# Per-token head attention: softmax along the free dimension, 32x32 block transposes, and score products with two tokens stationary

## The reference

```python
x = x + clip(layer0(x * style0) * demod0 + bias0, -256, 256)
kx = layerK(x)                       # reshaped to 16 heads of 32
scores = einsum("bnhd,bnjd->bnhj", kx, kx) / sqrt(32)
A = softmax(scores, axis=-1)
out = einsum("bnhj,bnjd->bnhd", A, kx)
x = x + layerO(out)
```

## Time and profile before

| | us |
|---|---|
| median of three runs | 892.17 |
| lowest and highest of them | 884.9, 893.84 |
| the profiled execution | 884.66 |
| its span, first to last instruction | 882.9 |
| TensorE busy in it | 820.0 |

### The profile page before, as it was taken

One profiled execution on the slowest core, in us unless ns is written; L12 is line 12 of the kernel. 1 busy time (PEld: TensorE's weight loads), 2 busy tenths in 40 slices (PEclk: granted clock), 3 DMA queues, 4 the chain that ended last, 5 costly groups with the idle time before them and its releaser, 6 DMA issues.

```text
span 882.9 us, 25721 instructions
## 1 busy us (share of the span) xinstructions
PE 820.0 (93%) x11024; PEld 794.0 (90%) x11024; DVE 613.6 (70%) x1224; ACT 548.3 (62%) x1077; POOL 11.6 (1%) x8
## 2 busy tenths in 40 slices
PE   5977989899999999999999999999999999997764
PEld 5976979899999999999999999999999999996664
DVE  4634675877787778778777877777777787774351
ACT  3433555666667767677666777666776667763452
POOL 3100000000000000000000000000000000000000
PEclk9888999999999999999999999999999999999788
DMA  8034366566666666666665666666666666654323
GB/s 267 25 90 100 79 147 157 142 160 160 141 149 145 145 157 164 161 147 165 150 160 129 165 138 148 159 161 164 144 161 153 155 134 160 139 125 107 73 73 119
DMA packets 471233, 123.95 MB, mean 140 GB/s; under 512 B 403152, under 2 KB 468816, under 8 KB 471120
## 3 DMA queue, kind: packets, MB, share of 16 engines
q1 hardware_dynamic: 471120, 122.31, 57.0%
HBM read 55.16 MB, written 50.33 MB: 119 GB/s over the span
## 4 chain that ended last, share of the span: by engine, by line
PE 80%; DMA 7%; DVE 4%; SPq 3%; ACT 3%; issue 1%; ACTq 0%; DVEq 0%
PE lin_ps L367 56%; PE s_ps L407 14%; PE y_ps L429 6%; PE cd_ps L414 3%; SPq L257 2%; DMA k_turned<-kx 2%; DMA yr<-y_turned 2%; DMA k_bd<-k_rhs 2%; DMA k_st<-k_turned 1%; PE y_ps L390 1%; SPq L265 1%; DVE k_rhs L701 1%; ACT y L548 1%; ACT y_hi L474 1%; PE y_ps L378 1%
## 5 line engine op out<-in xcount | busy, mean ns | idle before, releaser
L367 PE MATMUL lin_ps<-x_hi,w_hi 128*128 128x256 f32 x1024 | 297.6, 291 | 9.2 <-DVE x_lo L651 4.8
L367 PE MATMUL lin_ps<-x_lo,w_hi 128*128 128x256 f32 x1024 | 293.1, 286 | 0.0
L367 PE MATMUL lin_ps<-x_hi,w_lo 128*128 128x256 f32 x1024 | 292.9, 286 | 0.0
L367 PEld LDWEIGHTS lin_ps<-x_hi,w_hi 128*128 128x128 f32 x1024 | 199.5, 195 | 17.4 <-issue 11.6
L367 PEld LDWEIGHTS lin_ps<-x_lo,w_hi 128*128 128x128 f32 x1024 | 199.7, 195 | 1.6
L367 PEld LDWEIGHTS lin_ps<-x_hi,w_lo 128*128 128x128 f32 x1024 | 199.8, 195 | 0.0
L651 DVE SCALAR_TENSOR_TENSOR x_lo<-x,style,x_hi 128x256 fp32r<-128x256 f32 x256 | 111.8, 480 | 80.8 <-ACT x_hi L474 80.8
L367 PE MATMUL lin_ps<-y_hi,w_hi 128*128 128x256 f32 x512 | 148.2, 289 | 14.3 <-DVE y_lo L651 14.3
L407 PE MATMUL s_ps<-k_rhs,k_bd 128*64 128x48 f32 x4096 | 136.3, 226 | 12.0 <-DMA k_bd<-k_rhs 9.5
L367 PE MATMUL lin_ps<-y_lo,w_hi 128*128 128x256 f32 x512 | 147.3, 288 | 0.0
L367 PE MATMUL lin_ps<-y_hi,w_lo 128*128 128x256 f32 x512 | 146.9, 287 | 0.0
(11 more groups left out here) (58 smaller groups left out, 812.4 us busy)
## 6 DMA issues: line engine op xcount, KB each, us to landing
x<-xT SPq DMA_DIRECT2D x32, 512.0 KB, 5.3
k_turned<-kx SPq DMA_DIRECT2D x32, 512.0 KB, 3.7
k_st<-k_turned SPq DMA_DIRECT2D x128, 128.0 KB, 2.9
k_bd<-k_rhs SPq DMA_DIRECT2D x128, 128.0 KB, 4.0
y_turned<-y SPq DMA_DIRECT2D x128, 128.0 KB, 2.5
yr<-y_turned SPq DMA_DIRECT2D x32, 512.0 KB, 5.4
outT<-o SPq DMA_DIRECT2D x31, 512.0 KB, 2.9
p_bd<-wT SPq DMA_DIRECT2D x4, 512.0 KB, 7.2
```

The source lines that it names most:

```text
L367: mm = pe.matmul(lin_ps[:, n % NLB, 0:T], w[:, k, m * P:(m + 1) * P], r[:, k, :], start=(q == 0), stop=(q == len(passes) - 1))
```

## The change

**Scores.** Two tokens of each of four token blocks are stationary: 32 columns of k_rhs. The streaming operand is two tokens of the four parts of k_bd, 128 columns. Four such products fill the four groups of 32 partitions of one PSUM bank. The identity columns are gone. k_bd now holds its four parts one after the other, so a partition of a part is one run. Half of the computed 16x16 blocks belong to unlike tokens; ScalarE takes the even groups times a mask, and VectorE adds the odd groups times another mask, which leaves 16 scores in a row of sc.

**Softmax.** Maximum, subtraction, exponential, sum, reciprocal and multiplication run along the row of 16. Then a 32x32 block transpose on VectorE brings the probabilities into the layout of the products. The products of TensorE with ones, the splits and the corrected reciprocal are gone. The eight masked copies are four on VectorE and four on ScalarE in all chunks.

**Values.** k_rhs goes to DRAM and back in four transfers (`v_to_dram`, `v_from_dram`), and two block transposes on VectorE turn it into v_sb (`turn_v`).

**Order.** The accumulators of the linear layers get a fourth bank. The lists of all engines are written anew: SyncE's round, the place of turn_k, of the evacuation of y and of the next chunk's high and low parts. In the head layer L0 of chunk 3 is ahead of the scores of chunk 0. Three small constant inputs are no longer loaded.

```diff
         def pe_steps(i):
-            return (blocks(L0, i, [0, 1]) + one("max", i - 2) + blocks(L0, i, [2, 3])
-                    + blocks(O, i - 4, [0, 1]) + one("sum", i - 2) + blocks(O, i - 4, [2, 3])
-                    + blocks(K, i) + score_units(i - 1) + one("pv", i - 2))
-
-
-        SHARED_P = N - 2
+            return blocks(L0, i) + blocks(O, i - 4) + blocks(K, i) + one("scores", i - 1) + one("pv", i - 2)
...
+            + blocks(K, 0, [1, 2, 3]) + blocks(L0, 2) + blocks(K, 1) + blocks(L0, 3) + one("scores", 0)
+            + blocks(K, 2) + one("scores", 1) + blocks(K, 3) + one("pv", 0) + blocks(L0, 4) + one("scores", 2)
+            + blocks(K, 4) + one("pv", 1) + blocks(O, 0) + one("scores", 3) + one("pv", 2))
...
+            blocks(L0, last) + blocks(O, last - 4, [0, 1]) + blocks(K, last) + one("scores", last - 1)
+            + one("pv", last - 2) + blocks(O, last - 4, [2, 3]) + blocks(O, last - 3) + one("scores", last)
+            + one("pv", last - 1) + blocks(O, last - 2) + one("pv", last) + blocks(O, last - 1) + blocks(O, last))
...
             def spread_k(c):
...
                 if c == 0:
                     sp.wait_ge(g_zero, 1)
                 sp.wait_ge(v_krhs, c + 1)
-                for tb in range(HR):
-                    sp.dma_start(k_bd[HD * tb:HD * (tb + 1), :, tb, :],
-                                 k_rhs[HD * tb:HD * (tb + 1), 0]).then_inc(ld_kbd, DMA)
+                for r in range(R):
+                    sp.dma_start(k_bd[HD * r:HD * (r + 1), r], k_rhs[HD * r:HD * (r + 1)]).then_inc(ld_kbd, DMA)
+
+            def v_to_dram(c):
+                sp.wait_ge(v_krhs, c + 1)
+                if c >= 2:
+                    sp.wait_ge(v_in_landed, DMA * CT * (c - 1))
+                sp.dma_start(v_dram[c % 2], k_rhs[:, :, :].rearrange("p w n -> p (w n)")).then_inc(v_out_landed, DMA)
+
+            def v_from_dram(c):
+                sp.wait_ge(v_out_landed, DMA * (c + 1))
+                if c:
+                    sp.wait_ge(v_v, c)
+                src = v_dram[c % 2].rearrange("(r d) (c s) -> d r c s", d=HD, c=CT)
+                for ct in range(CT):
+                    sp.dma_start(k_v[HD * ct:HD * (ct + 1)].rearrange("p r x n -> p r (x n)"),
+                                 src[:, :, ct]).then_inc(v_in_landed, DMA)
...
+            for i in range(DEPTH + 1, N):
+                k_to_dram(i - 1)
+                k_from_dram(i - 1)
+                y_to_dram(i - 3)
+                y_from_dram(i - 3)
+                if i < N - 2:
                     load_x(i + 2)
-                if i >= 1:
-                    k_to_dram(i - 1)
-                    k_from_dram(i - 1)
-                if i >= 3:
-                    y_to_dram(i - 3)
-                if i >= 1:
-                    spread_k(i - 1)
-                if i >= 3:
-                    y_from_dram(i - 3)
-                if 3 <= i < N - 2:
-                    load_x(i + 2)
-                if DEPTH <= i < last:
+                spread_k(i - 1)
+                v_to_dram(i - 1)
+                if i < last:
                     store(i - 4, 0, 1)
+                v_from_dram(i - 1)
...
-                for q in range(GJ):
-                    for u in range(2):
-                        g = j * W + 2 * q + u
-                        mm = pe.matmul(s_ps[64 * u:64 * u + 64, j % 2, q * NC:(q + 1) * NC],
-                                       k_bd[:, g].rearrange("p b n -> p (b n)"), k_rhs[:, :, g, :], start=True, stop=True)
...
+            def scores(c):
+
+                pe.wait_ge(ld_kbd, DMA * R * (c + 1))
+                if c:
+                    pe.wait_ge(v_sc, c)
+                for x in range(2):
+                    for q in range(QS // 2):
+                        for ct in range(CT):
+                            w = (ct * 2 + x) * QS + 2 * q
+                            mm = pe.matmul(s_ps[HD * ct:HD * (ct + 1), x, q * P:(q + 1) * P],
+                                           k_rhs[:, w:w + 2].rearrange("p w n -> p (w n)"),
+                                           k_bd[:, :, w:w + 2].rearrange("p r w n -> p r (w n)"),
+                                           start=True, stop=True)
...
             def pv(c):
                 pe.wait_ge(v_pbd, c + 1)
-                if c >= SHARED_P:
-                    pe.wait_ge(a_pbd, c - SHARED_P + 1)
+                pe.wait_ge(a_pbd, c + 1)
+                pe.wait_ge(v_v, c + 1)
                 if c == 0:
                     pe.wait_ge(a_norm, 3)
-                for q in range(GJ):
-                    if q % PB == 0 and c:
-                        pe.wait_ge(a_y, NPB * (c - 1) + q // PB + 1)
-                    for j in range(HR):
-                        grp = j * GJ + q
+                else:
+                    pe.wait_ge(a_y, 2 * c)
+                for q in range(QS):
+                    for j in range(4):
+                        hi, x = j // 2, j % 2
+                        grp = ((x * QS // 2 + q // 2) * 2 + hi) * 2 + q % 2
                         mm = pe.matmul(y_ps[HD * j:HD * (j + 1), q // PB, (q % PB) * P:(q % PB + 1) * P],
-                                       sv_sb[:, c % 2, grp, HEADS:NC],
+                                       v_sb[:, c % 2, j * QS + q],
...
+            def even_scores(c):
+                if c == 0:
                     act.wait_ge(v_wlo, 6)
                     act.wait_ge(g_wsq, 2)
-                act.wait_ge(pe_s, SU * c + j + 1)
-                act.activation(sv_sb[:, c % 2, j * GJ:(j + 1) * GJ, :],
-                               s_ps[:, j % 2, 0:GJ * NC].rearrange("p (g n) -> p g n", n=NC),
-                               ACT.Copy).then_inc(a_sv, 1)
-
-            def evacuate_y(c, k):
-                if c and k == 0:
+                    act.wait_ge(v_odd, 1)
+                else:
+                    act.wait_ge(v_pt, c)
+                act.wait_ge(pe_s, c + 1)
+                act.activation(sc[:], s_ps[:, :, :].rearrange("p x (g o n) -> p (x g) o n", o=2, n=HEADS)[:, :, 0],
+                               ACT.Copy, scale=odd_mask[:, 0:1]).then_inc(a_even, 1)
+
+            def evacuate_y(c, l):
+                if c and l == 0:
                     act.wait_ge(y_out_landed, DMA * HR * c)
-                act.wait_ge(pe_pv, NPB * c + k + 1)
-                act.activation(y_sb[:, :, :, k * 2 * PB:(k + 1) * 2 * PB].rearrange("p h b w -> p w b h"),
-                               y_ps[:, k, :].rearrange("p (w b h) -> p w b h", b=HR, h=HEADS),
+                act.wait_ge(pe_pv, c + 1)
+                act.activation(y_sb[:, :, l].rearrange("p h (c q) -> p h c q", c=CT),
+                               y_ps[:, :, :].rearrange("p b (q c l h) -> p l h c (b q)", c=CT, l=2, h=HEADS)[:, l],
...
             def spread_some(c):
 
-                act.wait_ge(v_prob, c + 1)
-                act.wait_ge(pe_pv, NPB * c)
+                act.wait_ge(v_pt, c + 1)
+                act.wait_ge(pe_pv, c)
                 for t in range(TG // 2, TG):
-                    a = act.activation(p_bd[:, :, t, :], prob[:], ACT.Copy, scale=tok_mask[:, t:t + 1])
+                    a = act.activation(p_bd[:, :, t, :], p_turned[:], ACT.Copy, scale=tok_mask[:, t:t + 1])
...
+                    (c3, evacuate_y, 0), (c3, evacuate_y, 1), (c0, l0_out, 0), (c2, exponentials), (c0, l0_out, 1),
+                    (c0, l0_out, 2), (c2, spread_some), (c0, l0_out, 3), (c0, x1_hi_of, 0),
+                    (c4, o_out, 0), (c0, x1_hi_of, 1), (c4, o_out, 1), (i + 1, x_hi_of, 0),
+                    (c4, o_out, 2), (i + 1, x_hi_of, 1), (c4, o_out, 3),
+                    (c0, k_out, 0), (c3, y_hi_of, 0), (c0, k_out, 1), (c3, y_hi_of, 1), (c0, k_out, 2),
+                    (c0, k_out, 3), (c1, even_scores)]
...
             def turn_k(c):
-                dve.wait_ge(k_in_landed, DMA * HR * (c + 1))
+                dve.wait_ge(k_in_landed, DMA * R * (c + 1))
                 if c:
-                    dve.wait_ge(pe_s, SU * c)
-                dve.tensor_copy(k_rhs[:, 0], k_st[:, :, :].rearrange("p n w -> p w n")).then_inc(v_krhs, 1)
+                    dve.wait_ge(pe_s, c)
+                    dve.wait_ge(v_out_landed, DMA * c)
+                dve.tensor_copy(k_rhs[:].rearrange("p (c x q) n -> p c x q n", c=CT, x=2),
+                                k_st[:].rearrange("p n (x c q) -> p c x q n", x=2, c=CT)).then_inc(v_krhs, 1)
+
+            def turn_v(c):
+                if c == 0:
+                    dve.wait_ge(g_wsq, 2)
+                    dve.wait_ge(v_wlo, 6)
+                dve.wait_ge(v_in_landed, DMA * CT * (c + 1))
+                if c >= 2:
+                    dve.wait_ge(pe_pv, c - 1)
+                for hi in range(2):
+                    v = dve.transpose(v_sb[:, c % 2, hi * NG // 2:(hi + 1) * NG // 2],
+                                      k_v[:, 2 * hi:2 * hi + 2].rearrange("p l x n -> p x l n"))
+                v.then_inc(v_v, 1)
...
+            def merge_scores(c):
```

(35 more changed lines are left out.)

331 lines of the change are left out of this document (123 added, 208 removed).

## The result

The changed kernel takes 829.28 us (median of four runs, 827.42 to 835.37) against 891.1 (884.9 to 893.84), a ratio of 0.9327 with a 95% interval of 0.9255 to 0.9399. It is 7% faster. The forecast was 755 with a range of 730 to 800, so half of the gain that I counted on is missing, and the time lies outside the range. The profiled execution took 827.42 us, with a span of 825.6.

What follows compares the result with a forecast made beforehand. TensorE was taken to bound the middle of the run. Span 882.9 less 77 (25 rounds), 27.6 (head) and 28 (tail) gave 750, with 1.8 for execution 752, with scatter 755 us; range 730 to 800.

Steps and rivals of the forecast that it cites:

- walk through a round: Middle rounds, timed from TensorE's first linear layer: all hand-overs just fit; 0.1 us for small waits makes the round 21.25 us.
- the sum of SyncE's queue: SyncE's serial queue in a middle round: issues and landings sum to 20.4 us, under TensorE's 21.16.
- the landing of the spread: Spread of k into k_bd: first issue at 12.8 us, last landed near 16.8, wanted by the scores at 17.2.
- a late start is caught up before the spread: SyncE's queue: a late start does no harm, because k has landed by about 7 us and is wanted at 11.6.
- rival (b): Spread of k in the rounds: k_bd stays late, 1.9 us a round more, giving 802 us; chance 0.08.
- TensorE's own round: Middle rounds: TensorE's 24.34 us less 2.26 for scores and 0.92 for maxima and sums, 21.16 us.
- VectorE's transposes: Softmax and values on VectorE: three 32x32 transposes a round at 0.69 us each, 2.07 in all.
- Rival (a): Coupled middle round: a step of the walk about 1 us later, 1.2 us a round, 785 us; chance 0.22.
- (c): VectorE: a transpose costs many times a copy; at 4.5 us each, 934 us, slower than before; chance 0.02.
- (d): Scores on TensorE don't shrink: 2.2 us a round and 16 at the ends more, 825 us; chance 0.04.
- the identity in k_rhs: Head: writing it stands on the chain for 3.88 us, which go; counted as 3.9 of 27.6 us saved.
- the tail: After the rounds: walk of the last chunk gives 71 us, taken as 72 instead of 99.9, so 28 saved.

Runs made afterwards that it cites:

- experiment 3: Changed kernel with the spread of k issued for chunk 0 only, later scores computed from chunk 0's k_bd; 760.73 us (one run).
- experiment 6: Changed kernel with v loads one round later, load of x behind the spread of k, and copy of k early in VectorE's round; 763.43 us, ratio 0.860.
- experiment 2: Changed kernel with the four v loads of a chunk issued one round later in SyncE's queue, behind the next chunk's k out; 773.88 us, ratio 0.8742.
- experiment 7: Changed kernel with only VectorE's copy of k moved ahead of the second half of x1, SyncE's list untouched; 833.66 us, ratio 0.9366.
- experiment 10: Kernel of experiment 6 with SyncE's head list rewritten: y of chunk 0 and k of chunk 4 sent as soon as they are there; 763.41 us, ratio 0.859.
- experiment 4: Changed kernel with v's round trip through DRAM made for the first two chunks only, later chunks turning old values; 763.77 us (one run).

## Why the prediction was wrong

**Where it failed.** Two terms of the walk through a round were too small, and the first made the second so. The first is the sum of SyncE's queue: "Four fours at 2.0, five single ones at about 0.5 and 9.9 of landings are 20.4 us, under 21.16 but close." Over the 25 rounds it measured 22.1, above TensorE's round. The landings were right, 9.8 us. The groups of four were not: all were priced by the one row of y at 2.00, and they took 1.96, 2.54, 2.61 and 2.24 on average, 9.35 instead of 8.0; 0.6 us more went between the issues. The trace of before would have warned: over its 25 rounds the k loads took 2.6 us and the y stores 2.15 on average, and with these for the four groups the sum is about 21.5, already over 21.16.

The second is the landing of the spread in "last landed near 12.8 + 1.5 + 2.5 = 16.8; scores want it at 17.2". The 2.5 is the median of y, taken as if it didn't depend on what else is in flight. It holds where the queue has paused ahead of the spread. In a queue without slack yr and x go out directly ahead of it, and its last transfer took 5.6 to 7.0 us. The start, 12.8, came true in every round. So "a late start is caught up before the spread" was right for the start, and wrong as a comfort: the pause ahead of the spread, which kept the landing short, was what was used up. I had put the right numbers side by side, 20.4 against 21.16, and should have seen that 4% of slack on a sum of guesses is none.

**What was missing beside it.** The price of a wait on TensorE. A late k_bd cost the wait itself (most of the 43.8 us in which TensorE is idle in the 25 rounds) and about 0.6 us a round of slow work behind it: 21.8 busy, where experiments 3 and 6 have 21.2 at clock 1.00. The rival (b), "k_bd stays late", had the place and nearly the size (1.9 us a round against 2.3), with 0.08. It named v's added traffic as one reason, and the late landing is nearer to that than to the form of the old spread; but the same traffic in another order (experiment 2) cost little. The queue, which decided the order in time, stood in my text as a comfort.

**What was right.** TensorE's own round: 21.16 predicted, 21.01 in experiment 3 and 21.10 in experiment 6. Scores and products start 1.77 us apart (457.73 to 459.50) where I took 1.88. VectorE's transposes: 0.69 taken, 0.687 and 0.712 measured. It isn't the 1.24 us of the estimate by elements from the bf16 row of the Trainium skill's "VectorE: DVE Perf Modes" (section "The three transpose paths"). VectorE's load was 17.0 predicted and 16.6 in the undisturbed round; ScalarE's 16.8 and 15.6, because y costs 0.595 and not the 1.12 that I kept. The copy of k was done 12.7 us into the round in all 25 rounds, where the walk had 12.7 to 13.0. The sums of both engines leave more than 4 us of TensorE's round. The rule on copies out of PSUM from the Trainium skill's "TensorEngine Tiling (Array Packing)" (section "Performance Considerations") did not bind, as these sums show. Rival (a) as a step of the walk that comes too late did not set the changed kernel's time, as experiment 7 shows, but it was there behind the queue: experiment 6 gained 13 us by it. Rivals (c) and (d) are refuted by the rows of the transposes and of the scores.

**The ends.** The head ended 10 us later than forecast and the tail 8 us. In the head, 3.88 us for the identity in k_rhs were to vanish. They did from VectorE, but K of chunk 0 was not done earlier: ScalarE takes its last block at 52.36, where it did so at 50.85 before. The stretches from the first linear layer behind 14.5 us to the end of that layer, before and after:

```profile
14.58:50.85 36.27, 35.95 (x268) 35.59 (x269) 24.36 (x32) 16.67 (x33) 10.64 (x3) 0.91 0.19 62
14.61:52.36 37.75, 37.75 (x268) 37.75 (x269) 22.34 (x32) 16.49 (x32) 10.84 (x3) 0.86 0.18 59
```

TensorE had been busy in 35.95 of these 36.27 us already, also beside the identity, so there was hardly a wait that its going could shorten. Now it is busy all the time, with the same work at a lower granted clock. A step on the chain that ended last is not time that another engine spends idle. The rest of the head's error stays open, since experiment 10 gained nothing in time.

In the tail the walk had the scores of the last chunk start 33.4 us after the rounds' end; they start 39.1 after it. The chain there:

```profile
774.88 2.92 DMA y_turned<-y
...
780.28 4.61 DMA k_bd<-k_rhs
...
784.94 3.69 PE s_ps L425 x64
```

The walk left out the first, the queue's wait for y to land, and took 2.5 for the second. The scores themselves take 3.69 behind a wait of 9 us, where I took 1.88. With this the scores end 7.5 us later than in the walk, nearly all of the tail's 8.

## What to carry to other kernels

A queue that issues transfers in order and waits for landings in between is an engine with a round of its own: add up its issues and its waits as one adds up TensorE, from the means of all their rows rather than from one row, and compare the sum with the round that the change will make, not with the old one. Where it has no slack, look not only for transfers that start late: here the wanted one started in time and landed late, since others went out directly ahead of it. When a change makes the bounding engine faster and adds a round trip through DRAM, try the dependent loads behind something that has to be issued anyway, one round later; here this gave more than a second queue. And test an edit against the bound: the early copy of k gave 0 and 13 us, depending on whether the queue had been put right first.

## What the runs showed of the hardware

The same four transfers of 128 KB, with one run of 4 KB a partition, landed in 2.2 to 7.8 us across the runs, depending on what was in flight around them, and took 2.4 to 4.0 us to issue. In the changed kernel the last of them took 2.5 to 3.5 us where over 2.1 us had passed since the last transfer ahead of them was issued, and 5.6 to 7.0 where it was under 0.8. The long runs are quicker to issue than the old 64-byte runs, 2.6 us for four against 5.0 on average. Whether they land quicker can't be read from the two medians, 3.9 and 4.0, because v's traffic came with them; without it (experiment 4) the median is 2.4, though in another order of the queue. A 32x32 block transpose of 512 f32 elements a partition takes 0.69 to 0.71 us on VectorE, like the two-input operation on them (0.692). Reading PSUM scattered and writing runs, instead of reading runs and writing scattered, takes ScalarE's copy of y from 1.12 to 0.595 us.
